# The third add of squares moved behind three steps of a table lookup, and sums of squares taken with 128 columns of ones

## The reference

```
h   = per-sample 32x32 mix of x (weights from an MLP on cond, softmax over 8 experts)
p   = h @ in_proj_w.T            # gate, x, B, C, dt
xBC = silu(causal 4-tap conv)
y   = scan over 32 steps, 64 heads in 8 groups of 8:  state = state*dA + dtx*B ; y = state.C ; + x*D
yn  = y * rsqrt(mean(y*y over the group's 512) + 1e-5) * norm_weight * silu(gate)
x   = x + yn @ out_proj_w.T
c   = grouped conv of x + context + bias
ffn = where(norm(c) > 64, c @ w_high.T, c @ w_low.T) + bias
out = x + ffn
```

## Time and profile before

| | before |
|---|---|
| median of 3 runs | 3630.59 us (3630.27 to 3633.4) |
| the profiled execution | 3630.59 us, its span 3628.8 us |
| mean granted TensorE clock | 0.989 of full speed |
| TensorE matmul busy | 3503.7 us, 97% of the span |
| TensorE weight loads busy | 2887.1 us, 80% |
| VectorE busy | 3122.8 us, 86% |
| ScalarE busy | 1460.5 us, 40% |
| GpSimd busy | 468.3 us, 13% |

### The profile page before, as it was taken

The page is one execution under the profiler, slowest core; times in us unless marked ns, Lnnn a source line. Parts: engine busy times, 40 slices in busy tenths (PEclk is TensorE's granted clock), DMA queues, the critical chain, the costliest instruction groups (busy, mean ns, idle before and its releaser), DMA issues. The chain is left out here.

```text
span 3628.8 us, 58906 instructions
## 1 busy us (share of the span) xinstructions
PE 3503.7 (97%) x19789; PEld 2887.1 (80%) x19789; DVE 3122.8 (86%) x4932; ACT 1460.5 (40%) x2215; POOL 468.3 (13%) x297
## 2 busy tenths in 40 slices
PE   3779999999999999999999999999999999997999
PEld 2568888888888888888888888888888888886888
DVE  7669999999999999999999999999999999997333
ACT  1534444444444444444444444444444444442111
POOL 2200011111100111110111111100111111001333
PEclk9889999999999999999999999999999999998999
DMA  2733335333533244333632363235423453334331
GB/s 93 315 128 116 127 119 185 123 127 121 182 131 127 109 163 156 127 115 111 208 127 104 116 208 126 111 116 185 142 104 124 147 181 115 118 127 119 102 93 55
DMA packets 220671, 490.26 MB, mean 135 GB/s; under 512 B 39595, under 2 KB 85067, under 8 KB 211043
## 3 DMA queue, kind: packets, MB, share of 16 engines
q1 hardware_dynamic: 217060, 489.10, 38.2%
q0 software_dynamic: 304, 0.82, 0.1%
q10 hardware_dynamic: 3280, 0.04, 0.1%
HBM read 320.51 MB, written 169.39 MB: 135 GB/s over the span
## 5 line engine op out<-in xcount | busy, mean ns | idle before, releaser
L743 PE MATMUL bank<-ht,wt 128*128 128x512 f32 x7680 | 1862.8, 398 | 5.9 <-DMA ht<-h_d 5.9
L743 PEld LDWEIGHTS bank<-ht,wt 128*128 128x128 f32 x7680 | 1429.6, 188 | 349.1 <-issue 17.1
L965 DVE SCALAR_TENSOR_TENSOR xc<-bank,cvw,xc 128x496 f32<-128x496 f32 (+2 forms) x1152 | 814.6, 716 | 53.0 <-ACT xc L880 10.9
L838 PE MATMUL bank<-wot,gy 128*128 128x512 f32 x3072 | 737.7, 396 | 0.0
L880 ACT ACTIVATE xc<-bank,cvb,cvw 128x512 f32<-128x512 f32 x384 | 299.5, 780 | 1006.9 <-PE bank L743 1006.9
L838 PEld LDWEIGHTS bank<-wot,gy 128*128 128x128 f32 x3072 | 567.3, 188 | 127.9 <-issue 11.0
L719 POOL TENSOR_TENSOR r<-rv,neg_half 128x4 f32<-128x4 f32 x64 | 89.8, 1403 | 2455.8 <-DVE rv L1053 2455.8
L987 DVE TENSOR_TENSOR m<-cbm,y 128x1024 f32<-128x1024 f32 x256 | 301.5, 1219 | 9.8 <-DVE cbm L981 3.9
L716 POOL TENSOR_TENSOR segr<-adts,mask_le 128x1024 fp32r<-128x1024 f32 x128 | 242.8, 1918 | 380.2 <-DVE adts L956 380.2
L870 ACT ACTIVATE gy<-z 128x512 fp32r<-128x512 f32 x256 | 162.1, 633 | 320.5 <-DVE z L1027 320.5
L862 ACT ACTIVATE xc<-xc 128x512 f32<-128x512 f32 x384 | 234.0, 625 | 90.8 <-DVE xc L965 90.1
(11 more groups left out here) (162 smaller groups left out, 3066.9 us busy)
## 6 DMA issues: line engine op xcount, KB each, us to landing
ht<-h_d SPq DMA_DIRECT2D x64, 2048.0 KB, 7.9
acc<-acc_d SPq DMA_DIRECT2D x64, 1024.0 KB, 7.3
wt_d<-wnext SPq DMA_DIRECT2D x128, 512.0 KB, 3.1
acc_d<-acc SPq DMA_DIRECT2D x64, 1024.0 KB, 4.3
wt<-wt_d SPq DMA_DIRECT2D x70, 512.0 KB, 8.4
stage<-in_L_attn_in_proj_w SPq DMA_DIRECT2D x106, 256.0 KB, 2.8
h_d<-ht_out SPq DMA_DIRECT2D x8, 2048.0 KB, 7.5
wot<-wt_d SPq DMA_DIRECT2D x28, 512.0 KB, 6.1
```

The lines of the kernel that those rows point to most:

```text
L743: ins = pe.matmul(pb[:, :], wt[:, n, l, k, :], ht[:, rr, k, :], start=(q == 0 and k == 0), stop=(q == 2 and k == KC - 1))
L838: ins = pe.matmul(bank[OUT[t]][:, :], gy[:, c, l, t * P:(t + 1) * P], wot[:, rr, c, :], start=(c == 0 and q == 0), stop=(c == CT - 1 and q ...
L965: ins = dve.scalar_tensor_tensor(dst, src, cvw[:, n, TAPS - 1 - k:TAPS - k], dst, ALU.mult, ALU.add)
```

## The change

It has two parts. The constant `NSQ`, the number of columns of ones with which squares are summed, goes from 2 to `P` = 128. And in VectorE's list the join of lc and ld moves ahead of add 2, and add 3 moves behind pair 4, pair 5 and the join of la and lc, with its number changed from 7 to 9; the join of lb and ld behind it loses its own number 9 and with it one increment of the counter `s_w8go`.

```diff
-NSQ = 2
+NSQ = P
...
                             low(CT - 1)
                             join(1, la, lb)
+                            join(1, lc, ld)
                             add_squares(2, 6)
-                            join(1, lc, ld)
-                            add_squares(3, 7)
                             pair(4, lb, 6)
                             pair(5, ld, 7)
                             join(2, la, lc)
-                            join(1, lb, ld, 9)
+                            add_squares(3, 9)
+                            join(1, lb, ld)
                             pair(6, lc, 10)
```

## The result

| | before | changed |
|---|---|---|
| median | 3630.43 us (3629.53 to 3633.4, 4 runs) | 3664.97 us (3662.59 to 3666.22, 4 runs) |
| ratio | | 1.0094, 95% interval 1.0082 to 1.0107 |
| span of the profiled execution | 3628.8 us | 3662.6 us |
| mean granted clock | 0.989 | 0.988 |
| TensorE / its weight loads / VectorE | 97 / 80 / 86% | 96 / 79 / 85% |

The changed kernel is slower by 0.94%. The forecast was 3667.5 us.

A forecast was written before the change was run, and what follows sets the result against it. TensorE was taken to set the second stage's pace. 63 rounds x 0.59 = 37.2 us, less 0.31 in the last, gave 36.9 on 3630.6: 3667.5 us. Its own range was 3661 to 3678, the wider one 3655 to 3687.

The forecast's parts named there:

- TensorE sets the pace in the second stage: Second stage, 64 rounds: VectorE waits 0.74 us a round for TensorE's scan matmuls, while TensorE's projections wait once, 5.9 us.
- Add 3 is 1.22 us later: VectorE, end of a round: add 3 done 1.22 us later, not 1.53, because 0.31 of waits come off.
- Cover of 0.60 us, then the wait: Add 3 ended 0.60 us before L832 on TensorE wanted it; L832's first load now starts 0.67 to 0.75 later.
- 0.13 us comes back in L832's loads: TensorE: L832's eight loads behind an idle TensorE take 0.88 us instead of 1.01, so chunk 3 starts 0.54 to 0.62 late.
- The columns cost nothing: L832 and L1257 with 128 columns instead of 2: loads set the step, taken as 0 us.
- Nothing later takes it up: Rest of the round: TensorE has no wait that could shrink and absorb the 0.59 us lateness of chunk 3.
- Rival D: L832's wait is met late without harm: TensorE's work trails its records or later slack returns the 0.59; 3631 us, 3%.
- The last round is 0.31 shorter: Last round of the second stage: nothing of TensorE's follows, VectorE's acc updates close it, so 0.31 us less.
- Rival A: TensorE's clock falls in the new gap: 3766 us if once a round, 3717 if in one of two; 6%.

## Why the prediction was right

- **TensorE sets the pace in the second stage.** Shown from both sides: 0.3 us a round off VectorE brings nothing (3631.01), 0.45 off TensorE brings 29 us (3600.60), and a further 0.62 us of lateness at L832, beyond the cover, costs 37 us. The forecast read it from who waits, not from who is busy. The Trainium skill (Perfetto Trace Analysis, Identifying the Most-Contended Engine) ranks the engines by such shares. By TensorE's weight loads against VectorE's occupancy, 82% against 92%, it would have named VectorE, which the runs do not bear out; its second measure for TensorE, the arithmetic done as a share of the peak, was not worked out here.
- **Add 3 is 1.22 us later.** Measured 1.22. That included the 0.31 us of waits that go; in the trace the idle time ahead of the adds is 0.0 us. The Trainium skill's statement that a semaphore costs nothing extra (VectorE: DVE Perf Modes, The DRAIN you can't avoid) does not hold here for a wait for the instruction just ahead: 0.76 and 0.78 us with it, 0.62 without.
- **Cover of 0.60 us, then the wait.** L832's first load is 0.67 us later, the low end of 0.67 to 0.75. The semaphore took 0.05 us (1537.23 to 1537.28), as in the earlier trace rows; I had leaned to the 0.13 of the earlier trace rows. This is the miss of 2.5 us as far as it can be told: 0.59 a round was forecast and 0.54 measured, and 63 x 0.05 = 3 us.
- **0.13 us comes back in L832's loads.** Measured 0.12, with 2 columns and with 128. It is the second load, as the forecast had it: it started 0.23 us behind the first before and starts 0.11 behind it now, and the steps from there are 0.11 in both.
- **The columns cost nothing.** Shown by the run with the columns alone.
- **Nothing later takes it up.** Shown by the kernel with add 3 one step later: 0.62 us more wait, 0.62 us more a round. Rival D, at 3%, had nothing for it in the runs.
- **The last round is 0.31 shorter.** From add 3's end to the updates of acc it was 3321.22 - 3314.79 = 6.43 us and is 3357.64 - 3352.73 = 4.91, so 1.52 less, which is 1.22 and 0.30: seen in one execution, not tested apart.
- **Rival A** was given 6% with the argument that the gap is half of the 1.41 us of the earlier trace rows and that 128 columns stream behind it. For the changed kernel the outcome was right, and for the reason given only in part: with order alone the clock held with two columns too (0.72 us of wait, 0.89 of matmuls). The columns matter only when the wait is longer, as the two kernels with add 3 one step later show. What activity exactly decides it is not settled by these runs.

## What to carry to other kernels

Ask of each instruction on a slack engine when the busy one needs its result. Here 0.60 us of cover made one join's place free and the next join's place cost 34 us, with no work added. Put steps that nobody waits for behind those that the bound engine waits for, and price small matmuls by the count of their instructions, not by their columns: 2 and 128 cost the same here. If such a wait cannot be avoided, look at the granted clock behind it.

## What the runs showed of the hardware that was not expected

- An fp32 matmul of 128 x 128 weights took the same time with 2 columns as with 128, 0.11 us for each of its two instructions; in one pass as fp32r there were half as many at the same 0.11 us (four loads in 0.44 us behind a wait).
- Two-column matmuls behind a wait can cost the clock where 128-column ones in their place did not: 1.33 us of wait and 0.89 us of matmuls, with 2 columns at 1.2 GHz behind it in 54 of 64 rounds, with 128 columns in none, 83 us apart.
- Eight fp32 loads behind an idle TensorE took 0.89 us to the next line and not the 1.01 behind a running row of 512-column matmuls. The whole difference is in the second load, 0.11 us behind the first and not 0.23.
